# A wavelet stage on one Trainium2 core: the tile products take the low band's taps, and the attention denominators are made once for all heads

## The reference, cut to what matters

```python
low = x                                        # [4, 1024, 256]
for _ in range(2):                             # analysis, 4 taps for each channel
    l = dwconv(low, h_filter)[:, ::2]
    h = dwconv(low, g_filter)[:, ::2]
    highs.append(h); low = l
low = linear_attention(low, 16)                # on [4, 256, 256]
for h, L in zip(reversed(highs), reversed(lens)):   # synthesis
    up_l, up_h = repeat(low, 2)[:, :L], repeat(h, 2)[:, :L]
    low = dwconv(up_l, h_synth) + dwconv(up_h, g_synth)
return layer_norm(x + low, norm_gamma, norm_beta)

# linear_attention, 16 heads of 16 channels: q = k = elu(h) + 1, v = h
kv  = einsum("bnhd,bnhe->bhde", k, v);  z = k.sum(axis=1)
num = einsum("bnhd,bhde->bnhe", q, kv)
den = einsum("bnhd,bhd->bnh", q, z)[..., None] + 1e-6
out = num / den
```

## Time and profile before

| | us |
|---|---|
| median of 3 runs | 2115.46 |
| lowest and highest | 2114.1, 2120.17 |
| the profiled execution | 2117.32 |
| its span, first to last instruction | 2115.5 |
| VectorE's work on the last tile starts | 1788.58 |

### The profile page before, as it was taken

How to read it: one execution, slowest core, us unless ns; L and a number is a source line. 1 busy time by engine, 2 the same in 40 slices (tenths; PEclk the granted TensorE clock), 3 DMA queues, 4 the chain that set the end, 5 groups by cost and what they waited for, 6 DMA issues and landing times. The chain is left out here.

```text
span 2115.5 us, 36921 instructions
## 1 busy us (share of the span) xinstructions
PE 1801.3 (85%) x11152; PEld 1139.9 (54%) x11153; DVE 1182.9 (56%) x2499; ACT 895.2 (42%) x1314; POOL 435.1 (21%) x570
## 2 busy tenths in 40 slices
PE   7889999999999999986499999999995887065772
PEld 4523444444444444363488888888884467035551
DVE  4578888888888888644711111111112897846224
ACT  3436666666666666743032333233231430030323
POOL 2210000000000000030023333333331000301782
PEclk9979999999999999998799999999998899585886
DMA  4511111111111111054433434443442000241444
GB/s 147 182 48 35 31 36 32 30 38 30 32 36 30 34 34 30 16 167 144 164 90 112 113 93 114 115 103 103 117 111 87 1 1 8 97 139 35 50 47 159
DMA packets 103317, 158.32 MB, mean 75 GB/s; under 512 B 20832, under 2 KB 79520, under 8 KB 97888
## 3 DMA queue, kind: packets, MB, share of 16 engines
q1 hardware_dynamic: 69712, 118.46, 17.3%
q0 software_dynamic: 22656, 24.51, 7.3%
q10 hardware_dynamic: 10896, 14.69, 2.0%
HBM read 123.15 MB, written 49.02 MB: 81 GB/s over the span
## 5 line engine op out<-in xcount | busy, mean ns | idle before, releaser
L548 DVE TENSOR_REDUCE unit_max<-ps_ring 128x1 f32<-128x512 f32 x1024 | 639.5, 684 | 68.7 <-PE ps_ring L423 62.5
L534 ACT ACTIVATE w<-ps_scores 128x1024 f32<-128x1024 f32 x512 | 503.6, 1022 | 263.4 <-PE ps_scores L500 260.5
L423 PE MATMUL ps_ring<-k_stack,q_stack 96*128 96x512 bf16 x1024 | 366.4, 392 | 21.3 <-POOL v_padded L386 9.5
L500 PE MATMUL ps_scores<-q_stack,k_stack 98*128 98x512 bf16 x1024 | 306.2, 380 | 2.6 <-ACT w L534 2.5
L1411 PE MATMUL m_ps_h<-m_xt,m_w 128*128 128x256 f32 x1248 | 278.1, 381 | 0.8 <-DVE m_xt L1462 0.8
L1423 PE MATMUL m_ps_y<-w,m_ht 128*128 x1248 | 275.8, 379 | 0.0
L445 PE MATMUL ps_o<-w,v_padded 128*32 128x256 f32 x4096 | 260.6, 383 | 0.0
L1411 PEld LDWEIGHTS m_ps_h<-m_xt,m_w 128*128 128x128 f32 x1248 | 238.7, 191 | 34.0 <-DVE m_xt L1462 1.2
L1423 PEld LDWEIGHTS m_ps_y<-w,m_ht 128*128 128x128 f32 x1248 | 234.2, 190 | 30.3
L423 PEld LDWEIGHTS ps_ring<-k_stack,q_stack 96*128 96x128 bf16 x1024 | 98.6, 96 | 262.2 <-DVE unit_max L548 178.0
L1443 ACT ACTIVATE m_ht<-m_ps_h,m_w 128x256 f32<-128x256 f32 x312 | 130.7, 470 | 144.4 <-PE m_ps_h L1411 144.4
(11 more groups left out here) (238 smaller groups left out, 1788.0 us busy)
## 6 DMA issues: line engine op xcount, KB each, us to landing
m_w<-in_w SPq DMA_DIRECT2D x39, 1028.0 KB
rows<-g_rows SPq DMA_DIRECT2D x16, 512.0 KB, 2.9
y<-sums SPq DMA_DIRECT2D x16, 512.0 KB, 7.7
q_parts<-qk_part SPq DMA_DIRECT2D x16, 384.0 KB, 3.4
k_parts<-qk_part SPq DMA_DIRECT2D x16, 384.0 KB, 3.8
q_stack<-q_parts SPq DMA_DIRECT2D x64, 96.0 KB
k_stack<-k_parts SPq DMA_DIRECT2D x64, 96.0 KB
xt<-in_xt ACTq DMA_DIRECT2D x8, 512.0 KB, 4.2
```

The lines of the kernel that those rows point to most:

```text
L423: nc.tensor.matmul(out[:, :], qs[0:STACK, u, qt * P:(qt + 1) * P], ks[0:STACK, u, half * HALF:(half + 1) * HALF], start=True, stop=True).t ...
L500: mm = nc.tensor.matmul(p_s[kt % 2][:, half * HALF:(half + 1) * HALF], ks[:, u, kt * P:(kt + 1) * P], qs[:, u, half * HALF:(half + 1) * HALF],
L534: nc.scalar.activation(pt[:, kt, :], p_s[kt % 2][:, :], ACT.Exp, scale=SCALE)\
L548: nc.vector.tensor_reduce(unit_max[:, u % 2, half, qt:qt + 1], src[:, :], axis=AX.X, op=ALU.max).then_inc(ring_used, 1)
```

## The change

The tile products take over the low band's five taps of the first level's synthesis: ScalarE makes five more diagonals for each block (`diag` 9 to 13, from the h_synth sums), and each of the four outputs of a tile is now three or two products from `high1` and as many from `low1`. With that `synthesis(b)`, `begin_synthesis(b)`, the identity products and the writes to `c.xe` and `c.xo` go, and tiles wait for `syn2_ready` instead of `syn1_ready`. VectorE's order becomes attention(0), attention(1), tiles(0), attention(2), tiles(1), attention(3), tiles(2), tiles(3).

The denominators are made once: `zm` holds, for each of the 8 pairs of batch and block, 128 x 64 values of which 8 columns are not zero, and `denominators()` accumulates eight products into one block of 64 rows (batch and head) x 256 positions in bank 4. VectorE adds 1e-6 and takes one reciprocal of 64x256, after the masks of kv and ahead of the high-band taps. `numerators(b)` spreads the 64 rows to the 128 channels of a block by a product with `spread` (64 x 128, ones), and ScalarE's `copy_inv(b)` takes them from PSUM to `inv`, from where `attention(b)` multiplies. GpSimd makes `spread` and clears `zm`.

The order on TensorE changes too: `denominators()` stands ahead of `make_high1(4)`, `numerators(0)` and `(1)` behind `make_high1(5)`, `numerators(2)` behind `make_high1(7)`, and `numerators(3)` behind tile 1. The second level's low band is stored in the attention tile `al` instead of a tile of its own.

```diff
@@ -1544,22 +1544,23 @@
         mem = Mem(nc, stack)
         fil = mem.sb("w_filters", [P, KC, 4, 4])
         fs = mem.sb("w_sums", [P, KC, 2, 5])
-        diag = mem.sb("w_diag", [P, KC, 9, P])
+        diag = mem.sb("w_diag", [P, KC, 14, P])
         blocks = mem.sb("w_blocks", [P, P])
         low1 = mem.sb("w_low1", [P, KC, B, L1 + 2])
         high1 = mem.sb("w_high1", [P, KC, B, L1 + 2])
-        low2 = mem.sb("w_low2", [P, KC, B, L2])
         high2 = mem.sb("w_high2", [P, KC, B, L2 + 2])
         q = mem.sb("w_q", [P, KC, B, L2])
         z = mem.sb("w_z", [P, KC, B])
         al = mem.sb("w_attn", [P, KC, B, L2 + 2])
+        low2 = al[:, :, :, 1:1 + L2]
         qt = mem.sb("w_qt", [P, B, KC, 2, P])
         kvm = mem.sb("w_kv", [P, B, KC, P])
-        zm = mem.sb("w_zm", [P, B, KC, P])
-        den = mem.sb("w_den", [P, KC, L2])
+        zm = mem.sb("w_zm", [P, B * KC, NH])
+        spread = mem.sb("w_spread", [NH, B * KC * P])
+        den = mem.sb("w_den", [NH, L2])
+        inv = [mem.sb(f"w_inv{u}", [P, KC, L2]) for u in range(2)]
         htt = mem.sb("w_ht", [P, B, KC, 2, P])
 
-        se, so = c.xe, c.xo
         banks = [mem.ps(f"w_ps{n}") for n in range(8)]
         loaded, order, made = mem.sem("w_loaded"), mem.sem("w_order"), mem.sem("w_made")
         diag_ready, sums_ready = mem.sem("w_diag_ready"), mem.sem("w_sums_ready")
@@ -1568,9 +1569,10 @@
         low1_begun, low1_ready = mem.sem("w_low1_begun"), mem.sem("w_low1_ready")
         low2_begun = mem.sem("w_low2_begun")
         syn2_begun, syn2_ready = mem.sem("w_syn2_begun"), mem.sem("w_syn2_ready")
-        syn1_begun, syn1_ready = mem.sem("w_syn1_begun"), mem.sem("w_syn1_ready")
         min_ready, exp_ready, q_ready = mem.sem("w_min"), mem.sem("w_exp"), mem.sem("w_q_ready")
         turned, qt_copied, ht_copied = mem.sem("w_turned"), mem.sem("w_qt_copied"), mem.sem("w_ht_copied")
+        z_cleared, z_spread = mem.sem("w_z_cleared"), mem.sem("w_z_spread")
+        den_made, inv_ready, inv_copied = mem.sem("w_den_made"), mem.sem("w_inv_ready"), mem.sem("w_inv_copied")
         kv_made, kv_ready, nd_made, nd_used = mem.sem("w_kv_made"), mem.sem("w_kv_ready"), mem.sem("w_nd"), mem.sem("w_nd_used")
         tile_made, tile_used = mem.sem("w_tile_made"), mem.sem("w_tile_used")
         PAIRS = TB // 2
@@ -1607,6 +1609,13 @@
                 pool.wait_ge(made, 2)
                 nc.gpsimd.affine_select(out=bl, in_=bl, compare_op=ALU.is_ge, fill=0.0, base=HD - 1,
                                         pattern=[[HD, P // HD], [0, HD]], channel_multiplier=-1).then_inc(made, 1)
+
+                nc.gpsimd.memset(spread[:, :], 0.0).then_inc(made, 1)
+                pool.wait_ge(made, 4)
+                sp_rows = spread[:, :].rearrange("p (h r) -> p h r", r=HD)
+                nc.gpsimd.affine_select(out=sp_rows, in_=sp_rows, compare_op=ALU.not_equal, fill=1.0, base=0,
+                                        pattern=[[-1, NH], [0, HD]], channel_multiplier=1).then_inc(made, 1)
+                nc.gpsimd.memset(zm[:, :, :], 0.0).then_inc(z_cleared, 1)
 
             @block.vector
             def _(dve):
@@ -1642,9 +1651,7 @@
                     for n in range(1, 4):
                         link(add_tap(low2[:, k, :, :], part(low1, n, L2, 2)(k), tap(0, n)(k)))
 
-                flat = low2[:, :, :, :].rearrange("p c b n -> p (c b n)")
-                qf = q[:, :, :, :].rearrange("p c b n -> p (c b n)")
-                v.tensor_scalar(qf, flat, 0.0, None, ALU.min).then_inc(min_ready, 1)
+                v.tensor_scalar(q[:, :, :, :], low2, 0.0, None, ALU.min).then_inc(min_ready, 1)
                 for f in range(2):
                     for n, taps in enumerate(SUMS):
                         for k in range(KC):
@@ -1654,14 +1661,19 @@
                                     v.tensor_tensor(dst, src, fil[:, k, 2 + f, taps[1]:taps[1] + 1], ALU.add))
                 last.then_inc(sums_ready, 1)
                 dve.wait_ge(exp_ready, 1)
-                v.scalar_tensor_tensor(out=qf, in0=flat, scalar=0.0, in1=qf, op0=ALU.max, op1=ALU.add)\
+                v.scalar_tensor_tensor(out=q[:, :, :, :], in0=low2, scalar=0.0, in1=q[:, :, :, :], op0=ALU.max, op1=ALU.add)\
                     .then_inc(q_ready, 1)
                 dve.wait_ge(q_ready, 1)
                 link(v.tensor_reduce(z[:, :, :], q[:, :, :, :], axis=AX.X, op=ALU.add))
                 dve.wait_ge(made, 3)
+                dve.wait_ge(z_cleared, 1)
+                heads = P // HD
+                for n in range(B * KC):
+                    b, k = n // KC, n % KC
+                    last = v.tensor_scalar(zm[:, n, n * heads:(n + 1) * heads], blocks[:, 0:P:HD], z[:, k, b:b + 1], None,
+                                           ALU.mult)
+                last.then_inc(z_spread, 1)
                 for b in range(B):
-                    for k in range(KC):
-                        v.tensor_scalar(zm[:, b, k, :], blocks[:, :], z[:, k, b:b + 1], None, ALU.mult)
 
                     dve.wait_ge(turned, 2 * b + 1)
                     v.tensor_copy(qt[:, b, :, :, :].rearrange("p c j n -> p (c j n)"), banks[2 * b][:, :])\
@@ -1673,7 +1685,9 @@
                         last = v.tensor_tensor(kvm[:, b, k, :], banks[b][:, k * P:(k + 1) * P], blocks[:, :], ALU.mult)
                     last.then_inc(kv_ready, 1)
 
-
+                dve.wait_ge(den_made, 1)
+                link(v.tensor_scalar(den[:, :], banks[4][0:NH, 0:L2], 1e-6, None, ALU.add))
+                v.reciprocal(den[:, :], den[:, :]).then_inc(inv_ready, 1)
 
                 dve.wait_ge(syn2_begun, 2 * KC)
                 even, odd = part(low1, 1, L2, 2), part(low1, 2, L2, 2)
@@ -1688,12 +1702,10 @@
                 def attention(b):
 
                     dve.wait_ge(nd_made, b + 1)
-                    n, d = 2 * (b % 2) + 4, 2 * (b % 2) + 5
-                    dn = den[:, :, :].rearrange("p c n -> p (c n)")
-                    link(v.tensor_scalar(dn, banks[d][:, :], 1e-6, None, ALU.add))
-                    link(v.reciprocal(dn, dn))
+                    dve.wait_ge(inv_copied, b + 1)
+                    n = 2 * (b % 2) + 4
                     v.tensor_tensor(al[:, :, b, 1:1 + L2], banks[n][:, :].rearrange("p (c n) -> p c n", c=KC),
-                                    den[:, :, :], ALU.mult).then_inc(nd_used, 1)
+                                    inv[b % 2][:, :, :], ALU.mult).then_inc(nd_used, 1)
                     dve.wait_ge(nd_used, b + 1)
 
                     even, odd = of_batch(low1, b, 1, L2, 2), of_batch(low1, b, 2, L2, 2)
@@ -1707,19 +1719,6 @@
                             link(last)
                     last.then_inc(syn2_ready, 1)
 
-                def synthesis(b):
-
-                    dve.wait_ge(syn1_begun, (b + 1) * 2 * KC)
-                    for n in (1, 2):
-                        for dst, terms in ((of_batch(so, b, 1, L1), ODD), (of_batch(se, b, 0, L1), EVEN)):
-                            for k in range(KC):
-                                if n < len(terms):
-                                    off, t = terms[n]
-                                    last = add_tap(dst(k), of_batch(low1, b, off, L1)(k), total(0, t)(k))
-                        if n == 1:
-                            link(last)
-                    last.then_inc(syn1_ready, 1)
-
                 def tiles(b):
                     for i in range(b * PAIRS, (b + 1) * PAIRS):
 
@@ -1732,13 +1731,11 @@
                             row_stats(nc, c, 2 * i + j)
 
 
-                for b in range(B + 2):
+                for b in range(B + 1):
                     if b < B:
                         attention(b)
-                    if 1 <= b <= B:
-                        synthesis(b - 1)
-                    if b >= 2:
-                        tiles(b - 2)
+                    if b >= 1:
+                        tiles(b - 1)
 
             @block.scalar
             def _(act):
@@ -1765,16 +1762,17 @@
                                          banks[4 + n][:, :].rearrange("p (b n) -> p b n", b=2), ACT.Copy)\
                         .then_inc(high2_copied, 1)
 
+                def copy_inv(b):
+
+                    act.wait_ge(nd_made, b + 1)
+                    wait_from(act, nd_used, b - 1)
+                    nc.scalar.activation(inv[b % 2][:, :, :].rearrange("p c n -> p (c n)"), banks[2 * (b % 2) + 5][:, :],
+                                         ACT.Copy).then_inc(inv_copied, 1)
+
                 def begin_low2(k):
                     act.wait_ge(low1_ready, k + 1)
                     first_tap(low2[:, k, :, :], part(low1, 0, L2, 2)(k), tap(0, 0)(k), low2_begun)
 
-                def begin_synthesis(b):
-
-                    act.wait_ge(syn2_ready, b + 1)
-                    for k in range(KC):
-                        first_tap(of_batch(so, b, 1, L1)(k), of_batch(low1, b, 1, L1)(k), total(0, 3)(k), syn1_begun)
```

(58 more changed lines are left out.)

## The result

| | before | after |
|---|---|---|
| median, us (13 runs each) | 2116.53 (2112.89 to 2120.17) | 2121.31 (2116.51 to 2125.56) |
| profiled execution: time, span, granted clock | 2117.32, 2115.5, 0.922 | 2117.61, 2115.8, 0.927 |

The account below looks back on a forecast made before the run. The prediction took TensorE's queue in the wavelet stage to set the kernel's end. Its terms, 21.4 + 3.5 - 0.3 - 18.9 = +5.7 us on a median of 2115.46 us, gave 2121.1 us, range 2117 to 2126 us.

Parts of the forecast that it names:

- What bounds the stage: Wavelet stage: TensorE's queue sets the end; VectorE's savings count only as far as they remove TensorE's idle time.
- The tiles, +21.4 us: TensorE's 16 tiles: from 28 to 40 records each at 0.1116 us a record, 4.46 us a tile, +21.4 us.
- Rival E: Tiles: a record costs less at the margin than on the mean; faster, 2105 us or so, chance 0.04.
- rival B: Slower tile pace (+7.9 us), or less to win because the clock stays up during a stop (+7.4 us); chance 0.20.
- The denominators, +3.5 us: TensorE: 16 new 256-column records add 3.5 us; spread products replace zm products at no change, 1.73 us a batch.
- rival D: 64-column products at the 128-column pace, or fewer cycles somewhere in TensorE's queue: +2 to +4 us, chance 0.08.
- Start of kv, -0.3 us: TensorE's kv products start at 1694.8 us, released by ScalarE's last copy: -0.3 us, bounds 0 and -0.3.
- All stops and slow tiles go, -18.9 us: TensorE from kv on: all four stops and both slow tiles vanish, first tile's data 4.2 us early; -18.9 us.
- Rival C: VectorE's wait for the denominators makes attention(0) late by more than 4.2 us: 2124 to 2128 us, chance 0.06.
- The clock rule: TensorE's clock falls only after stops of 4.6 us or more, none after 2.5 us; new tile phase at 2.4 GHz.
- The sum: Whole kernel: 21.4 + 3.5 - 0.3 - 18.9 = +5.7 us, 2121.1 us on the median; within 2 us, chance 0.62.
- GpSimd, 0 to +1 us: GpSimd's new clears and select might slow VectorE's first taps by 2 us, mostly covered by TensorE's high2: 0 to +1 us.

Follow-up runs that it names:

- e1: Changed kernel with the denominators' edit alone: synthesis and 14-product tiles of the kernel before; 2105.48 us, ratio to before 0.9945.
- e8: Changed kernel plus one scratch 128x512 reciprocal and its clear (3.9 us of VectorE) ahead of attention(0); 2122.71 us, ratio to before 1.0030.
- e3: Changed kernel with zm, spread and den padded from 64 to 128, so all products have 128 rows; 2120.82 us, ratio to before 1.0025.
- e4: Changed kernel plus three scratch 128x512 reciprocals on VectorE between the high-band taps and attention(0); 2126.89 us, ratio to before 1.0052.
- e6: Kernel before, unchanged, run and profiled a second time; 2116.93 us, ratio 0.9999.
- e5: e1 with the padding to 128 rows of e3; 2104.03 us, ratio to before 0.9945.
- e2: Kernel before with the changed tiles, diagonals and VectorE order, but its own denominators; 2122.14 us, ratio to before 1.0026.

## Why the prediction was right

**What bounds the stage: right.** TensorE's queue sets the end, VectorE's savings count for nothing beyond the stops. e1 and e8 show both sides: with VectorE's synthesis back but no long stop the stage is 11.6 us shorter from kv on, and with 3.9 us more on VectorE it is not longer at all.

**The tiles, +21.4 us: right.** 4.47 us a tile against 4.46; the marginal record costs what the mean one did. From tile 0 to last the changed kernel takes 23.5 us more than e1, 2.1 us of which are `numerators(3)`. Rival E and the pace half of rival B are out. The prediction's 0.107 us for a weight load is seen here as the distance between two loads in a row, 0.11 us (1704.96 to 1705.07 us); the record of one load is 0.19 us long.

**The denominators, +3.5 us: the mis-sized term.** The sixteen records took 3.59 us (1694.30 to 1697.89), as forecast, so rival D, which had them at 1.8 us, is out. What failed is the step "four spread products with 64 rows and the same 256 columns take their place: no change, 1.73 us a batch". The two groups of a batch took 2.12 us: 1709.10 less 1704.87, where the last 512-column pair would have handed over, is 4.23 us for two batches, against 3.45 us. That is 0.39 us a batch, 0.19 us for each of the eight changes between 64 and 128 rows, 1.55 us in all. Entering and leaving the 64-column products adds about 0.3 us (in the changed kernel against e3: 3.74 against 3.65 us for kv, 3.59 against 3.45 us for the sixteen records, 0.97 against 0.86 us for the first high1 pair behind them). e3 shows it by taking it back: 1.90 us. The step was given no bound. The stage before has no two shapes of different row counts in turn, but a later stage of the same trace does, and TensorE's timeline of before had a row for it:

```profile
1870.52 1.03 PE L888 MATMUL g_ps_logits_t<-g_rows_t,g_w 128*8 128x256 f32 x4
1871.48 0.61 PE L896 MATMUL g_ps_logits<-ident,g_logits_t 8*128 8x8 f32 x4
```

Four 256-column records with 128 rows hand over to a record with 8 rows after 0.96 us, where a group took 0.86 us: 0.1 us for the first side of a change (the weight columns change there too, from 8 to 128). So a price could have been read ahead of the edit.

**Start of kv, -0.3 us: right.** It is released by ScalarE's copy as forecast (L1795), and TensorE's stop ahead of it is 0.78 us in every kernel with the new order, 1.00 us in the others. The 39.18 against 39.51 us from clear to kv do not show it, since that time varied from 39.15 to 41.05 us.

**All stops and slow tiles go, -18.9 us: right for the changed kernel.** The first tile stands at 1718.09 us, 3 us earlier than the forecast 1721, but the stage began 4.2 us earlier: counted from kv it came after 27.53 us, forecast 26.1 (1720.9 less 1694.8), 1.4 us late by the shape changes ahead of it (26.01 us in e3). That made its slack larger than the 4.2 us of the forecast: e8's 3.9 us fitted in, and of e4's 10.1 us of reciprocals and some 0.5 us of clear 5.1 us showed as stops, which leaves about 5.5 us, 0.5 us of it VectorE's own wait for the inverse. The trace of the changed kernel says the same: attention(0)'s taps start at 1708.64 us and take 4.30 us, which ends them 5.1 us ahead of the first tile. Rival C is out.

**The clock rule: wrong.** "Here each fall to the lower level came after a stop of 4.6 us or more, none after 2.5 us" held for one execution. In e6 the stop of 2.49 us was followed by it, and in e4 it came 2 us behind the end of one of 2.97 us, while e1's 1.78 us and e5's 3.08 us were not followed by it. So what there was to win in the kernel before varies, 18.9 us in one profile and 19.6 in the other (94.23 less the 74.6 us of work). It went the other way from rival B, which gave before less to lose. That rival is not excluded for a timed run that has no profile.

**The sum.** From clear to last the changed kernel took 5.2 to 7.7 us more (140.49 and 140.67 against 133.00 and 135.28), forecast +5.7. The timed difference is 3.0 to 7.2 us. That the median agrees to 0.2 us is in good part luck:

- +1.8 us of shape changes are in the stage, and the prediction had nothing for them.
- Only the stage was argued, and the prediction took a shift of its end for a shift of the kernel's end. But in both profiles of the changed kernel the part behind the stage is 3.0 to 3.5 us shorter than in both of before (323.9 and 323.5 against 326.9 and 327.0 us). Over all ten executions it lies between 323.5 and 329.8 us. No run here separates its cause, so that stays open.
- The base, the median of three runs, was 1.1 us below the median of 13; with that one the forecast would have been 2122.2 us.

Whether before's lower clock ahead of kv in some executions offset some of this in the timed runs stays open too, since those have no trace.

**GpSimd, 0 to +1 us: right at 0,** though VectorE did feel it. Timelines of GpSimd and VectorE in the changed kernel:

```profile
1652.46 0.95 POOL L1613 MEMSET w_spread<- 64x1024 f32 x1
1653.56 2.30 POOL L1616 TENSOR_SCALAR_AFFINE_SELECT w_spread<-w_spread 64x1024 f32<-64x1024 f32 x1
```

```profile
1654.53 3.44 DVE L1633 SCALAR_TENSOR_TENSOR w_low<-x_even,w_filters,w_low 128x2048 f32<-128x2048 f32 x1
```

The tap beside the select took 3.44 us, where the same one took 2.35 us before. It took 2.35 us in e2 too, where GpSimd does not have the new work. TensorE's high2 products began 19.35 us after clear, before 19.48 us: nothing of it reached TensorE.

## What to carry to other kernels

When one change holds two edits, price each against what the other leaves: the stops were worth 18.9 us together, the denominators alone won 11.6 us of it from kv on, and the tile taps then paid 21.4 us of TensorE work for a last stop of 1.8 us. Moving work onto the engine that sets the end is only worth the idle time that it removes there, and that has to be counted after the cheaper edit is in. If two profiled spans seem to say that nothing happened, measure between marks of the stage itself, add up what lies ahead of them and behind them too, and profile the kernel before twice.

## What the runs showed of the hardware

- Each change between products of 64 and of 128 rows cost TensorE about 0.19 us (group start to group start 1.06 instead of 0.86 us), with the weight load no longer ahead of the matmul. With padding to 128 rows it was gone, though the array then multiplies zeros. Not every change of row count costs it: in the kernel's first stage bfloat16 products with 96 and with 98 rows alternate (L423, L500; starts at 137.75, 137.96, 138.18 and 138.40 us), and the steps between them are 0.22 us as within one shape.
- The granted clock fell during or within 0.3 us behind the stops of 6.47 and 4.62 us (before) and of 5.25, 5.62 and 2.49 us (e6), and 2 us behind one of 2.97 us (e4). It stayed up after 2.49 us in the first profile of before and in e2, after 1.78 us in e1 and after 3.08 us in e5. The length of a single stop did not decide it in these traces; what does stays open.
- TensorE's slow products at the start of the stage took 3.46 us in one execution of the kernel before and 6.49 us in another.
- The reciprocal on 64 rows and 256 columns took 1.75 us, as did e3's on 128 rows and 256 columns, against 3.35 us on 128 rows and 512 columns: its price went by the columns, as taken.
